# A graph-attention layer on one core: one scatter table for the ho edges instead of two, hh scatters in two steps, table loads on SyncE, and a new order of VectorE's work

## The reference

```python
h = relu(layernorm(x))
feat = concat(h[src], h[dst])                      # 8704 x 2048
e = relu(feat @ W_kind + b_kind)                   # hh: first 256 edges, oo: next 1280, ho: the rest
logit = e @ W_a + b_a
alpha = softmax of logit over the edges with the same dst
z[dst] += alpha * h[src]
h_new = relu(concat(h, z)[:128] @ W_hn + b_hn)
o_new = relu(concat(h, z)[128:] @ W_on + b_on)
out = x + concat(h_new, o_new)
```

## Time and profile before

| | us |
|---|---|
| median of 3 runs | 478.55 (477.81 to 479.96) |
| profiled execution, its time | 478.8 |
| its span, first to last instruction | 477.0 |
| PE busy | 446.9 (94%) |
| DVE busy | 343.0 (72%) |
| POOL busy | 260.4 (55%) |
| ACT busy | 156.2 (33%) |

### The profile page before, as it was taken

How to read it: one execution, slowest core, us unless ns; L and a number is a source line. 1 busy time by engine, 2 the same in 40 slices (tenths; PEclk the granted TensorE clock), 3 DMA queues, 4 the chain that set the end, 5 groups by cost and what they waited for, 6 DMA issues and landing times.

```text
span 477.0 us, 5094 instructions
## 1 busy us (share of the span) xinstructions
PE 446.9 (94%) x1782; PEld 323.2 (68%) x1788; DVE 343.0 (72%) x635; ACT 156.2 (33%) x228; POOL 260.4 (55%) x221
## 2 busy tenths in 40 slices
PE   1999999999999999999999996999999999994696
PEld 1788888887888688744444442665788888873584
DVE  5770442783978776747688877979996579969947
ACT  3920151334131315594556013014231422063210
POOL 2040000034788778777778778777875787615000
PEclk9999999999999999999999998699999999998599
DMA  8989842597886869697767668488855989226004
GB/s 335 371 316 422 324 178 88 199 325 250 288 276 224 291 209 304 205 325 254 238 213 226 199 215 275 136 310 280 312 184 176 340 305 369 60 88 228 36 2 177
DMA packets 39146, 113.95 MB, mean 239 GB/s; under 512 B 13593, under 2 KB 13593, under 8 KB 33360
## 3 DMA queue, kind: packets, MB, share of 16 engines
q1 hardware_dynamic: 12256, 58.83, 32.9%
q0 software_dynamic: 22592, 46.41, 30.7%
q10 hardware_dynamic: 4272, 8.39, 4.6%
HBM read 123.83 MB, written 17.86 MB: 297 GB/s over the span
## 4 chain that ended last, share of the span: by engine, by line
POOL 23%; PE 22%; issue 20%; DMA 16%; DVE 16%; ACT 2%; POOLq 0%; DVEq 0%
POOL gath L1090 8%; POOL gath L1097 7%; DMA pairs_ho_odd<-logit,cell 7%; PE bank L848 6%; PE bank L847 6%; PE bank L846 6%; POOL pairs_ho L1109 4%; POOL pairs_ho_odd L1109 3%; DMA gath<-q_ho,q_index 3%; DVE gath L586 3%; DMA pairs_ho<-logit,cell 3%; DMA gath<-q_oo,q_index 2%; DVE stage L786 2%; DVE gath L589 2%; DVE g_raw L531 1%
## 5 line engine op out<-in xcount | busy, mean ns | idle before, releaser
L846 PE MATMUL bank<-w_hi,h_t 128*128 128x512 f32 x432 | 172.1, 398 | 0.2 <-DVE g_raw L531 0.2
L847 PE MATMUL bank<-g_raw,h_t 128*128 128x512 f32 x432 | 169.3, 392 | 0.0
L848 PE MATMUL bank<-w_hi,h_t 128*128 128x512 f32 x432 | 169.3, 392 | 0.0
L586 DVE TENSOR_TENSOR gath<-gath 128x512 f32<-128x512 f32 x132 | 85.6, 689 | 58.4 <-DMA gath<-q_ho,q_index 45.7
L1090 POOL DMA_INDIRECT gath<-p_ho,i_src x56 | 68.8, 1228 | 77.0 <-DMA p_ho<-stage 59.9
L297 ACT ACTIVATE w_hi<-raw 128x1024 fp32r<-128x1024 f32 x56 | 56.3, 1062 | 139.3 <-PE bank L848 50.8
L846 PEld LDWEIGHTS bank<-w_hi,h_t 128*128 128x128 f32 x432 | 82.0, 190 | 21.5 <-issue 4.5
L848 PEld LDWEIGHTS bank<-w_hi,h_t 128*128 128x128 f32 x432 | 81.8, 189 | 17.2
L847 PEld LDWEIGHTS bank<-g_raw,h_t 128*128 128x128 f32 x432 | 81.9, 190 | 16.8 <-issue 0.5
L531 DVE TENSOR_TENSOR g_raw<-raw,w_hi 128x512 fp32r<-128x512 f32 x112 | 70.0, 686 | 27.8 <-ACT w_hi L297 27.6
L589 DVE SCALAR_TENSOR_TENSOR gath<-gath,wa 128x1024 f32<-128x1024 f32 x66 | 80.9, 1226 | 2.3
(11 more groups left out here) (146 smaller groups left out, 329.0 us busy)
## 6 DMA issues: line engine op xcount, KB each, us to landing
raw<-w_chunks SPq DMA_DIRECT2D x40, 1024.0 KB, 6.1
gath<-x SPq DMA_DIRECT2D x4, 512.0 KB, 4.8
h_dram<-h_sb SPq DMA_DIRECT2D x1, 2048.0 KB, 11.6
p_ho<-stage ACTq DMA_DIRECT2D x2, 1024.0 KB, 6.3
p_oo<-stage ACTq DMA_DIRECT2D x2, 1024.0 KB, 8.1
q_oo<-stage ACTq DMA_DIRECT2D x2, 1024.0 KB, 7.4
x_again<-x SPq DMA_DIRECT2D x2, 1024.0 KB, 6.2
out<-partial SPq DMA_DIRECT2D x8, 256.0 KB, 2.0
```

What stands on the lines that cost most here:

```text
L586: i = nc.vector.tensor_tensor(p[:, cols], p[:, cols], q[:, cols], ALU.add)
L846: nc.tensor.matmul(to, hi, w_high, start=first, stop=False)
L847: nc.tensor.matmul(to, hi, w_low, start=False, stop=False)
L848: return nc.tensor.matmul(to, lo, w_high, start=False, stop=last)
```

## The change

It makes one ho table of two: all 56 ho scatters go into pairs_ho, each behind a wait for the landing of the one before it. The oo tables stay two. The elementwise maximum of the ho tables, one table to clear and two loads go with it. The hh scatters move forward to the turns n = 49 and n = 51, one in each. The loads of the hh and the ho table are issued by SP, behind its last load of weights. POOL no longer adds the exponentials; DVE adds them after the multiplications. On ACT `split_hi(39)` goes ahead of the exponentials, and `evacuate_sums(2)` and `(3)` ahead of `split_hi(27)`. DVE's order is written anew. The diff, cut to its core:

```diff
-HH_AT = 57
+HH_STEPS = (49, 51)
...
         @block.sync
-                    for kind in (("ho_odd", "oo"), ("oo_odd", "hh"))[c - RAW]:
+                    for kind in (("oo", "oo_odd"), ("hh",))[c - RAW]:
                         clear(kind)
+            sp.wait_ge(s_hhscat, 16 * T_HH)
+            sp.wait_ge(s_diff, 4)
+            sp.dma_start(tab_sb[2], pair_tab["hh"].rearrange("(b p n) o -> p b (n o)", p=P, n=N)).then_inc(s_tab[2], 16)
+            sp.wait_ge(s_scat[0], 16 * T_HO)
+            sp.wait_ge(s_pst, 64)
+            sp.dma_start(tab_sb[0], pair_tab["ho"].rearrange("(b p n) o -> p b (n o)", p=P, n=N)).then_inc(s_tab[0], 16)
...
         @block.scalar
-            act.wait_ge(s_oused, 32)
-            split_hi(27)
             evacuate_sums(2)
             evacuate_sums(3)
+            split_hi(27)
...
             split_hi(38)
+            split_hi(39)
             exps(0, 1, 4)
             exps(2, 1, 4)
-            split_hi(39)
...
         @block.vector
             tiles(3)
-            unpack(2, 0, pair_steps, step_sums[:, 0], True)
-            split_lo(27)
-            tiles(1)
             weigh_hh(1)
             nc.vector.tensor_tensor(logit_hh[:, :], logit_half[:, 0], logit_half[:, 1], ALU.add).then_inc(s_hhlog, 1)
+            split_lo(27)
+            tiles(3)
+            unpack(2, 0, pair_steps, step_sums[:, 0], True)
+            split_lo(29)
+            tiles(3)
+            split_lo(31)
+            tiles(2)
+            split_lo(32)
             tiles(1)
-            split_lo(29)
-            tiles(4)
-            split_lo(31)
+            split_lo(33)
             tiles(1)
-            split_lo(32)
-            tiles(2)
             unpack(3, 2, step_sums[:, 0], step_sums[:, 1], False)
             tiles(1)
-            split_lo(33)
-            tiles(2)
...
             split_lo(34)
             tiles(2)
             split_lo(35)
-            tiles(1)
+            tiles(2)
             split_lo(36)
             tiles(1)
             g_lo(0)
-            tiles(1)
+            tiles(2)
             split_lo(37)
             tiles(2)
+            split_lo(38)
             dve.wait_ge(s_tab[2], 16)
             table_peak(2, pk_hh)
-            split_lo(38)
             tiles(1)
             g_lo(1)
-            tiles(1)
-            dve.wait_ge(s_tab[0], 48)
-            for a in range(2):
-                i = nc.vector.tensor_tensor(tab_sb[0][:, 2 * a:2 * a + 2], tab_sb[0][:, 2 * a:2 * a + 2], ho_odd[a],
-                                            ALU.max)
-            step(i)
+            dve.wait_ge(s_tab[0], 16)
...
-                i.then_inc(s_weighed, 1)
+            step(i)
+            for b in ORDER:
+                i = nc.vector.tensor_tensor(tab_sb[0][:, b], tab_sb[0][:, b], tab_sb[2][:, b], ALU.add)
+            step(i)
...
         @block.gpsimd
-                kind, odd = "ho" if n < T_HO else "oo", n % 2
-                table = odd if kind == "ho" else 2 + odd
-                landed = (n if kind == "ho" else n - T_HO) // 2
+                kind, table, landed = ("ho", 0, n) if n < T_HO else (("oo", "oo_odd")[n % 2], 1 + n % 2, (n - T_HO) // 2)
                 pool.wait_ge(s_logit, n + 1)
                 if landed:
                     pool.wait_ge(s_scat[table], 16 * landed)
...
-                if n == HH_AT:
-
-                    pool.wait_ge(s_hhlog, 1)
-                    for e in range(T_HH):
-                        if e:
-                            pool.wait_ge(s_hhscat, 16 * e)
+                if n in HH_STEPS:
+                    e = HH_STEPS.index(n)
+                    if e == 0:
+                        pool.wait_ge(s_hhlog, 1)
+                    else:
+                        pool.wait_ge(s_hhscat, 16 * e)
...
-                if n == HH_AT + 1:
-                    pool.wait_ge(s_hhscat, 16 * T_HH)
-                    pool.wait_ge(s_diff, 4)
-                    load_table(2)
-                if n == T_HO + LAG + 1:
-
-                    for side in range(2):
-                        pool.wait_ge(s_scat[side], 16 * (T_HO // 2))
-                    load_table(0)
-                    load_ho_odd()
-            for n, b in enumerate(ORDER):
-                pool.wait_ge(s_weighed, n + 1)
-                nc.gpsimd.tensor_tensor(tab_sb[0][:, b], tab_sb[0][:, b], tab_sb[2][:, b], ALU.add).then_inc(s_esums, 1)
```

More of the change, by code:

```diff
@@ L101, in build @@
                 "oo": (dram("p_oo", (N, D)), dram("q_oo", (N, D)))}
-    pair_tab = {k: dram(f"pairs_{k}", (N * N, 1)) for k in ("ho", "oo", "hh", "ho_odd", "oo_odd")}
+    pair_tab = {k: dram(f"pairs_{k}", (N * N, 1)) for k in ("ho", "oo", "hh", "oo_odd")}
     with ExitStack() as ctx:
@@ L185, in build @@
         tab_sb = [stage[:, 0], gath[:, 0, 0:2, :].rearrange("p a (b n) -> p (a b) n", n=N), stage[:, 1]]
-        ho_odd = [gath[:, a, SLOTS - 1].rearrange("p (b n) -> p b n", n=N) for a in range(2)]
         oo_odd = gath[:, 0, 2:4, :].rearrange("p a (b n) -> p (a b) n", n=N)
@@ L207, in build @@
         s_esum, s_logit = sem("edge_summed"), sem("logit_ready")
-        s_scat = [sem("even_ho_scattered"), sem("odd_ho_scattered"), sem("even_oo_scattered"), sem("odd_oo_scattered")]
+        s_scat = [sem("ho_scattered"), sem("even_oo_scattered"), sem("odd_oo_scattered")]
         s_node = sem("node_row_ready")
@@ L211, in build @@
         s_hhhalf = sem("hh_half_logits")
-        s_weighed, s_esums = sem("early_exps_weighed"), sem("early_exps_summed")
         s_part = sem("partial_ready")
@@ L258, in _ @@
                 if c < RAW + 2:
-                    for kind in (("ho_odd", "oo"), ("oo_odd", "hh"))[c - RAW]:
+                    for kind in (("oo", "oo_odd"), ("hh",))[c - RAW]:
                         clear(kind)
+            sp.wait_ge(s_hhscat, 16 * T_HH)
[4 more added lines that the diff above has]
+            sp.dma_start(tab_sb[0], pair_tab["ho"].rearrange("(b p n) o -> p b (n o)", p=P, n=N)).then_inc(s_tab[0], 16)
             for odd in range(2):
-                sp.wait_ge(s_scat[2 + odd], 16 * (T_OO // 2))
+                sp.wait_ge(s_scat[1 + odd], 16 * (T_OO // 2))
                 sp.wait_ge(s_logit, T_NODE - 1 + odd)
@@ L332, in evacuate_q @@
                 else:
-                    act.wait_ge(s_tabs, 80)
+                    act.wait_ge(s_tabs, 64)
                 for b in range(NB):
@@ L594, in _ @@
             dve.wait_ge(s_bias, 16)
-            dve.wait_ge(s_tabs, 80)
+            dve.wait_ge(s_tabs, 64)
             evacuate_p(0, 0, 0)
@@ L813, in _ @@
                 step(nc.vector.tensor_tensor(tab_sb[1][:, b], tab_sb[1][:, b], counts[:, 1, b], ALU.mult))
-                dve.wait_ge(s_esums, n + 1)
                 nc.vector.scalar_tensor_tensor(out=att[:, b], in0=tab_sb[0][:, b], scalar=drop_exp[:, b:b + 1],
@@ L1076, in _ @@
                                                  ).then_inc(s_hh_rows, 16)
[L1078 to L1086, removed]
             def p_rows(n):
@@ L1108, in scatter @@
                     pool.wait_ge(s_scat[table], 16 * landed)
-                nc.gpsimd.indirect_dma_start(pair_tab[kind + ("", "_odd")[odd]][:, :], bass.IndirectOffsetOnAxis(ap=cell[:, at:at + 1], axis=0),
+                nc.gpsimd.indirect_dma_start(pair_tab[kind][:, :], bass.IndirectOffsetOnAxis(ap=cell[:, at:at + 1], axis=0),
                                              logit[:, at:at + 1], None).then_inc(s_scat[table], 16)
-            pool.wait_ge(s_tabs, 80)
+            pool.wait_ge(s_tabs, 64)
             pool.wait_ge(s_norm, 2)
@@ L1125, in _ @@
                     pool.wait_ge(s_qst, Q_STORES[4])
-                if n == HH_AT:
-                    pool.wait_ge(s_hhlog, 1)
-                    for e in range(T_HH):
-                        if e:
-                            pool.wait_ge(s_hhscat, 16 * e)
-                        nc.gpsimd.indirect_dma_start(pair_tab["hh"][:, :],
-                                                     bass.IndirectOffsetOnAxis(ap=pair_hh[:, e:e + 1], axis=0),
-                                                     logit_hh[:, e:e + 1], None).then_inc(s_hhscat, 16)
+                if n in HH_STEPS:
[4 more added lines that the diff above has]
+                        pool.wait_ge(s_hhscat, 16 * e)
+                    nc.gpsimd.indirect_dma_start(pair_tab["hh"][:, :],
+                                                 bass.IndirectOffsetOnAxis(ap=pair_hh[:, e:e + 1], axis=0),
+                                                 logit_hh[:, e:e + 1], None).then_inc(s_hhscat, 16)
                 if SLOTS <= n < T_NODE:
```

## The result

The changed kernel takes 515.32 us (median of 4 runs, 511.87 to 518.84) against 478.18 us (476.96 to 479.96) of the kernel before on the same chip: ratio 1.077, interval 1.068 to 1.087. The profiled execution took 517.55 us with a span of 515.7. It is slower, as forecast, but by 37 us where 16 were forecast, and the time lies outside the range.

The account below looks back on a forecast made before the run. POOL's pace up to the 60th tile's rows, then DVE's own work, set the end: 389.3 - 5.7 + 25 = 408.6, + 32.4 + 3.4 = 444.4 (+16.7), then -0.7: span 493.0, time 494.5 us, range 484 to 504, chance 0.70.

Parts of the forecast that it names:

- The one-step rule: POOL's ho scatters: each may start only when the previous one has landed; forecast 25 us of added waits over 55 scatters.
- what DVE does itself behind it: DVE from the 60th tile's start to the last tile's end: 32.4 us of own work forecast, against 38.4 before.
- Counting PE's 3.7 us at zero: PE's wait for ACT's copy of the sums goes, but PE isn't on the path setting the end: no gain counted.
- The overhead behind a landing is small: I take 0.27 us, a gap like those between POOL's instructions.: On POOL, between an awaited landing and the next scatter's start: 0.27 us assumed.
- Together 6.05 us for eleven, 0.55 us a scatter: POOL's added waits summed over eleven ho landings named by the chain of waits, scaled to 30 us for 55 scatters.
- upper bound of 37: Most added waits on POOL, in us, were there another landing like the longest: 44 us, less a sixth.
- The sixth taken off for neighbours that overlap: POOL's added waits cut from 30 to 25 us, as one transfer often holds up two neighbouring scatters.
- The wait for the rows of a later tile: DVE waits once for tile 63's gathered rows, behind the 60th tile: 3.4 us, between 0 and 5.
- Rival 1: Landings shorten when POOL pauses, at most 5.7 us of added waits, DVE's gain stays: 472 us; chance 0.11.
- rival 2: POOL's added waits are only 10 to 15 us, just paid for by the savings: 478.5 us; chance 0.07.
- Rival 3: Starved DVE makes PE's last chunk end after DVE's attention; with 37 us of waits, 506 us; chance 0.12.
- Rival 4: SP's loads come so late that DVE waits for the hh table; stays in the forecast's range, no separate chance.

Follow-up runs that it names:

- b_one_ho: The kernel before with only the ho tables merged into one, each ho scatter waiting for the landing of the one before: 518.08 us, ratio 1.087.
- a_two_ho: The changed kernel with two ho tables again (SP loading both, DVE taking their maximum), all else as changed: 470.9 us, ratio 0.979.
- b_hh_steps: The kernel before with the hh scatters at turns n = 49 and n = 51, nothing else: 471.94 us, ratio 0.989.
- a_two_sums: The changed kernel with two ho tables and with the sums copied out behind split 27 on ACT again: 472.36 us, ratio 0.988.
- a_swap: The changed kernel with the scatter's two waits, for logits and for the last landing, in the other order: 502.98 us, ratio 1.055.
- after: The changed kernel itself, with all parts of the change, against the kernel before: 515.32 us, ratio 1.077.
- b_hh_39: The kernel before with hh scatters at turns 49 and 51 and split 39 ahead of the exponentials on ACT: 474 us, ratio 0.991.

## Why the prediction was right in kind and wrong in size

**Right: the mechanism.** The one-step rule makes POOL wait (b_one_ho 41 us by itself, a_two_ho none), the waits come to the end through POOL's late gathers of rows around the 60th tile, and what DVE does itself behind it is as long as forecast. From 427.75 to 465.6 are 37.9 us, less the row wait of 5.54 makes 32.3; the prediction had 32.4. Multiplying and adding took 7.4 us, forecast 7.5. The hh steps gave 5.4 us, forecast 4.9 without the load of the hh table, which stayed on POOL in b_hh_steps. Counting PE's 3.7 us at zero can't be tested in the changed kernel; with two tables it does not hold (a_two_sums).

**Wrong: the size of the added waits.** Up to the 52nd scatter the prediction's terms give 0.455 us of waits a turn (25 / 55), 23 us for 51 turns, and the two hh scatters of 1.28 us each that now lie ahead of it: 354.86 + 23.2 + 2.6, which it gave as "near 380". It was 400.84. From first to 52nd scatter the changed kernel takes 279.45 us against 235.0; less 2.6 for hh that leaves 41.9 us of loss. (POOL stood 47.8 us longer ahead of these scatters than the usual 0.30; its own instructions took 6.1 us less in all, and 41.9 is about what is left.) Two steps of the prediction failed:

- *"The overhead behind a landing is small: I take 0.27 us, a gap like those between POOL's instructions."* It was 0.77 us, in every wait of over 1 us. With the landing's wait attached to the scatter (a_swap) it was exactly 0.27, and the time fell by 11 to 12 us. The rows of before that the 0.27 came from are of instructions that wait for nothing, or, at the second hh scatter, for one thing alone; the ho scatter of the changed kernel has two waits ahead of it, and it is the one for the landing that is issued apart. This is 12.7 of the 18.7 us (41.9 - 23.2) that were missing.
- *"Together 6.05 us for eleven, 0.55 us a scatter".* The eleven landings were those that the chain of waits happened to name, and they are shorter than the rest: 4.20 us in the mean, against 4.63 for all 56 in the same trace. The same sum over the 51 turns up to the 52nd scatter, still with 0.27 us, is 38.7 us, 0.76 a turn, and 40.4 for 55 scatters, more than the upper bound of 37. It was there to be worked out before the result was known.

The sixth taken off for neighbours that overlap was not the fault. In a_swap, where the overhead was as assumed, the waits up to the 52nd scatter were 386.95 - 120.16 - 235.0 - 2.6 = 29.2 us, a quarter less than the 38.7. That the plain sum over the eleven (0.55 x 51 = 28.1) comes so near to 29.2 is luck: a sample that was too low stood against an overlap that was left out. In terms of the sum: 23.2, and 9.0 more with all landings in place of eleven, 3.0 less with a quarter off in place of a sixth, 12.7 more for the overhead, make 41.9. So the second step is worth 6 us net. Whether it is the overlap that takes the quarter is not shown.

With the first scatter 1.5 us later than before, that is all of the 20 us at the 52nd scatter, and 19.1 us at the start of tile 60 (427.75 against 408.6).

**Wrong, and small.** The wait for the rows of a later tile was 5.54 us, not 3.4, and it stood at the 61st tile and not at the 63rd. And behind the last tile, 1.5 us more than forecast, where DVE stood 2.86 us for ACT. In the sum: 19.1 + 2.1 + 1.5 = 22.7 us of span, 515.7 against 493.0.

**The range.** Its upper bound of 37 us for the waits was built from the sample of eleven and took the overhead as known. All 56 landings with 0.27 us and a sixth off would have given 32.3 us up to the 52nd scatter, inside the range. The unknown that hurt most was the one that had no bound: a duration (0.27) read from instructions that wait for nothing was used for one that waits.

**The rivals.** Rival 1 (the waits hide) and rival 2 (half of it) fell. Rival 3 (PE joins in) was there in part: PE waits for DVE around 300 to 360 us at a granted clock of 0.78, PE's last two chunks start behind `g_lo(1)` and stand in the chain that ended last, as that rival has it, and DVE waits for what comes behind them. But beside DVE's own chain this is worth 1.5 us or so of the end, not 12. Rival 4 (SP's loads too late): no wait of DVE for a table stands in after, so it did not happen.

**The rule of the Trainium skill** (DMA: Bandwidth & Descriptors, section Anatomy of one DMA), about 2.0 us for a transfer as small as a scatter's, had pointed to rival 1. The shortest landings agree with it:

```profile
330.46 2.43 DMA pairs_ho<-logit,cell
```

But the mean of after was 4.17 us and the longest over 7. By the rule no turn would have waited; here 23 did. The rule has no term for other traffic, and beside a load of weights the trace of after has 5.7 us.

**What stays open.** Why a separate wait costs half a microsecond more than an attached one is not shown, only that it does, each time. What split 39 adds to the 10 us of a_two_ho is not settled (1.2 us by the medians, 4 by the ratios); the sums' part is some 4.5 us, with 3.6 us of noise. And of the long landings it is shown that loads of weights make most of them, not by which step of the transfer.

## What to carry to other kernels

Two tables (or buffers) written in turn are not waste when a small write shares the DMA engines with large loads: price the one-step rule by the landing next to a load, turn by turn, and not by the shortest or the mean one. When a wait is added, look which instruction carries it: of two waits ahead of an indirect DMA, write first the one that will really wait, and take the overhead from a row that waits. Where the trace has every landing, take the sum over all of them, with the wait of each turn worked out, and not over those that a chain of waits happens to name. And when two numbers agree, look whether two errors stand against each other.

## What the runs showed of the hardware that was not expected

- Two waits ahead of a POOL indirect DMA: the one that the code has last becomes an instruction of its own, the other goes with the DMA. From the awaited landing to the DMA's start are 0.77 us when the landing is awaited by the separate one (after), 0.27 us when it is awaited by the DMA itself (a_swap), with no variation over 24 and 17 waits.
- The landing of a 512-byte scatter of 128 cells: 2.9 us in the mean away from a 1 MB load, 5.7 us beside one (after). Cutting eight such loads out of the way gave back 15 us.
- 3.57 us of idle time on the engine of the end can be worth nothing if another chain ends level with it: the same time then stands as 3.26 us of waiting a few instructions on (b_hh_39).
